# Attention heads laid out as two 64-row tensor tiles in place of zero-padded full-height tiles, with the maxima units regrouped by side

## The reference

```python
x = x + 0.5 * ffn(layernorm(x), ...)      # mixture of 8 experts, top 2, capacity 1.25
x = x + attn(layernorm(x), ...)           # below
x = x + 0.5 * ffn(layernorm(x), ...)      # the same experts again

def attn(x, wq, bq, wk, bk, wv, bv, wo, bo):          # x: (4, 1024, 128)
    q, k, v = (split(x @ w.T + b) for w, b in ...)    # 16 heads of width 8
    scores = einsum('bhsd,bhtd->bhst', q, k) / 8 ** 0.5
    scores = where(causal, scores, -inf)
    ctx = einsum('bhst,bhtd->bhsd', softmax(scores), v)
    return ctx.transpose(0, 2, 1, 3).reshape(B, S, E) @ wo.T + bo
```

## Time and profile before

| | us |
|---|---|
| median of three runs | 1189.49 |
| the profiled execution, span from first to last instruction | 1184.2 |
| median of the runs less that span | 5.3 |
| attention sweep with maxima (first scores of group 0 to first scores of group 15) | 380.7 to 907.7 |
| busy in the whole span: PE / DVE / ACT / POOL | 900.6 / 636.2 / 487.1 / 553.3 |

### The profile page before, as it was taken

How to read it: one execution, slowest core, us unless ns; L and a number is a source line. 1 busy time by engine, 2 the same in 40 slices (tenths; PEclk the granted TensorE clock), 3 DMA queues, 4 the chain that set the end, 5 groups by cost and what they waited for, 6 DMA issues and landing times. The chain is left out here.

```text
span 1184.2 us, 21961 instructions
## 1 busy us (share of the span) xinstructions
PE 900.6 (76%) x7525; PEld 560.8 (47%) x7525; DVE 636.2 (54%) x1515; ACT 487.1 (41%) x767; POOL 553.3 (47%) x645
## 2 busy tenths in 40 slices
PE   2320899992048999999999799999999622999980
PEld 2320677872023454555555355555554211878770
DVE  6440333331358878878777587787876130333230
ACT  1000343340021676568645477555766301443430
POOL 2775277767510322133427234163323632577776
PEclk9999999997566999999999899999999855999995
DMA  4212676733152114131152302422200113454522
GB/s 146 66 53 84 186 187 158 179 63 28 27 158 47 43 29 149 43 79 45 32 149 67 80 18 58 136 76 63 61 17 13 46 35 113 81 114 69 87 25 19
DMA packets 101649, 92.59 MB, mean 78 GB/s; under 512 B 15348, under 2 KB 80017, under 8 KB 101521
## 3 DMA queue, kind: packets, MB, share of 16 engines
q1 hardware_dynamic: 73024, 71.71, 21.8%
q0 software_dynamic: 27136, 17.09, 10.1%
q10 hardware_dynamic: 1392, 2.51, 0.7%
HBM read 48.32 MB, written 47.12 MB: 81 GB/s over the span
## 5 line engine op out<-in xcount | busy, mean ns | idle before, releaser
L1235 DVE TENSOR_REDUCE m_units<-banks 128x2 f32<-128x512 f32 (+1 forms) x576 | 381.1, 688 | 94.3 <-PE banks L954 78.6
L1184 ACT ACTIVATE pt<-banks 128x1024 f32<-128x1024 f32 (+3 forms) x384 | 291.4, 809 | 163.3 <-PE banks L937 161.4
L954 PE MATMUL banks<-kp,qa 128*128 128x256 bf16 (+1 forms) x1536 | 229.3, 254 | 17.7 <-DMA kp<-k_stack 10.3
L1444 POOL TENSOR_SCALAR_AFFINE_SELECT pt<-pt 128x512 f32<-128x512 f32 x128 | 81.6, 638 | 256.9 <-ACT pt L1184 256.7
L937 PE MATMUL banks<-qb,kp 128*128 128x512 bf16 (+3 forms) x768 | 188.6, 329 | 7.2 <-issue 5.1
L954 PEld LDWEIGHTS banks<-kp,qa 128*128 128x128 bf16 x1536 | 119.5, 99 | 148.7 <-DVE m_units L1235 59.5
L983 PE MATMUL banks<-pt,vs 128*32 128x256 f32 (+2 forms) x2560 | 178.5, 371 | 6.1 <-POOL pt L1444 6.0
L648 ACT ACTIVATE hT<-banks,bfc 128x512 f32<-128x512 f32 (+1 forms) x192 | 113.8, 615 | 168.4 <-DVE bfc L666 94.3
L722 POOL DMA_INDIRECT mid<-ys,ids x80 | 124.9, 1561 | 70.2 <-issue 34.4
L342 POOL DMA_INDIRECT bucket<-rows,row_ix x128 | 125.7, 982 | 64.2 <-issue 38.2
L722 POOL DMA_INDIRECT out_dram<-ys,ids x80 | 123.7, 1546 | 67.8 <-DVE ys L691 32.8
(11 more groups left out here) (166 smaller groups left out, 643.1 us busy)
## 6 DMA issues: line engine op xcount, KB each, us to landing
bucket<-zero SPq DMA_DIRECT2D x16, 660.0 KB, 4.2
xb<-bucket SPq DMA_DIRECT2D x16, 660.0 KB, 4.7
q_stack<-qp SPq DMA_DIRECT2D x24, 256.0 KB, 3.0
k_stack<-kq SPq DMA_DIRECT2D x24, 256.0 KB, 3.7
qa<-q_stack SPq DMA_DIRECT2D x32, 192.0 KB, 3.5
kp<-k_stack SPq DMA_DIRECT2D x32, 192.0 KB, 4.4
qb<-q_stack SPq DMA_DIRECT2D x32, 192.0 KB, 3.4
wfc<-in_L_ffn_c_fc_dram SPq DMA_DIRECT2D x16, 256.0 KB, 3.0
```

Source lines behind the costliest of these rows:

```text
L954: i = nc.tensor.matmul(a_bank[a % 2][:, j * w:(j + 1) * w], qa[par][:, h, qt * P:(qt + 1) * P], kp[g][:, h // 2, k0:k0 + w], start=not dia ...
L1184: nc.scalar.activation(pt[u % PTS][:, 2 * pair:2 * pair + 2, 0:w], two[pair][:, :, 0:w], ACT.Exp, scale=SCALE).then_inc(exp_done[pair], 1)
L1235: nc.vector.tensor_reduce(m_units[:, qt, at, heads[0]:heads[-1] + 1], a_bank[a % 2].rearrange("p (h k) -> p h k", k=w), AX.X, ALU.max).the ...
L1444: nc.gpsimd.affine_select(out=v, in_=v, compare_op=ALU.is_ge, fill=0.0, base=0, pattern=[[0, HS], [1, P]], channel_multiplier=-1).then_inc ...
```

## The change

- `qa` and `qb` hold two slabs (one per pair) where they held four. Side `s` of slab `i` is head `2i + s`, on partitions `64 s` and up. Nothing is zero-padded, and the four clears of `qa` and `qb` are gone.
- `score` and `maxima` take 51 or 48 rows, from partition 0 or 64, in both operands: each matmul is on one of two 64-row tiles. Banks, widths and the order of the blocks in a slot stay.
- A maxima unit has one side only: heads 0, 2 or heads 1, 3. A 256-key unit is two matmuls as before. The 128-key units and the diagonal units take two query tiles of one side where they took four heads of one query tile. The number of units stays 36, `A_IN_SLOT` stays, but the diagonal units now come last in each half. The reduce writes 2 heads of 1 or 2 query tiles.
- The transfers that fill `qb` from the maxima rows and `qa`, `qb` from the stacks keep their number and size; only the head order and the slab layout change.

```diff
+    HB = T // 2
     for hf in (1, 0):
-        for qt in range(hf * T // 2, (hf + 1) * T // 2):
+        qts = range(hf * HB, (hf + 1) * HB)
+        for qt in qts:
             for j in range(qt // 2):
-                AUNITS += [(qt, (0, 1), 2 * j * P, 2 * P, False, j), (qt, (2, 3), 2 * j * P, 2 * P, False, j)]
-            if qt % 2:
-                AUNITS.append((qt, range(HS), (qt - 1) * P, P, False, T // 2 - 1))
-            AUNITS.append((qt, range(HS), qt * P, P, True, T // 2))
+                for side in range(2):
+                    AUNITS.append((hf, side, [(qt, 2 * j * P)], 2 * P, False, j))
+        for side in range(2):
+            AUNITS.append((hf, side, [(qt, (qt - 1) * P) for qt in qts if qt % 2], P, False, HB - 1))
+        for q2 in range(hf * HB, (hf + 1) * HB, 2):
+            for side in range(2):
+                AUNITS.append((hf, side, [(q2, q2 * P), (q2 + 1, (q2 + 1) * P)], P, True, HB))
...
-            qa = [sba(f"qa{i}", [P, HS, S], bf16) for i in range(2)]
-            qb = [sba(f"qb{i}", [P, HS, S], bf16) for i in range(2)]
+            qa = [sba(f"qa{i}", [P, HS // 2, S], bf16) for i in range(2)]
+            qb = [sba(f"qb{i}", [P, HS // 2, S], bf16) for i in range(2)]
...
-                        i = nc.tensor.matmul(two[pair][:, s, 0:w], kp[g][:, pair, kb * P:(kb + 1) * P],
-                                             qb[par][:, 2 * pair + s, q0:q0 + w], start=True, stop=True)
+                        rows_s = slice(64 * s, 64 * s + KS + 3)
+                        i = nc.tensor.matmul(two[pair][:, s, 0:w], kp[g][rows_s, pair, kb * P:(kb + 1) * P],
+                                             qb[par][rows_s, pair, q0:q0 + w], start=True, stop=True)
...
-                        for j, h in enumerate(heads):
-                            i = nc.tensor.matmul(a_bank[a % 2][:, j * w:(j + 1) * w], qa[par][:, h, qt * P:(qt + 1) * P],
-                                                 kp[g][:, h // 2, k0:k0 + w], start=not diag,
-                                                 stop=not diag or j == len(heads) - 1)
+                        rows_s = slice(64 * side, 64 * side + KS)
+                        todo = [(qt, k0, pair) for qt, k0 in segs for pair in range(HS // 2)]
+                        for j, (qt, k0, pair) in enumerate(todo):
+                            i = nc.tensor.matmul(a_bank[a % 2][:, j * w:(j + 1) * w],
+                                                 qa[par][rows_s, pair, qt * P:(qt + 1) * P],
+                                                 kp[g][rows_s, pair, k0:k0 + w], start=not diag,
+                                                 stop=not diag or j == len(todo) - 1)
...
-                nc.vector.memset(qa[0][:], 0.0)
                 norm(0)
-                for t_ in qa[1:] + qb:
-                    i = nc.vector.memset(t_[:], 0.0)
-                i.then_inc(cleared, 1)
```

More of the change, by code:

```diff
@@ L830, in load_q @@
                 def load_q(dst, b, g, done):
-                    load_stack(lambda s: dst[64 * s:64 * s + KS].rearrange("p (i s) n -> p s i n", s=2)[:, s],
-                               q_stack, b, g, done)
+                    load_stack(lambda s: dst[64 * s:64 * s + KS], q_stack, b, g, done)
                 def load_k(b, g):
@@ L880, in move @@
                     for s in range(2):
[L881 to L884, removed]
+                        src = max_rows[hf * 3 * HS:(hf + 1) * 3 * HS, :].rearrange("(c s i) n -> s c i n", c=3, s=2)[s]
+                        dst = qb[par][64 * s + KS:64 * s + KS + 3]
+                        sp.dma_start(dst[:, :, hf * HALF:(hf + 1) * HALF], src).then_inc(max_ld[hf][par], 16)
                 def store_stacks(b):
@@ L914, in _ @@
                 wait_apart(sp, stack_st, STORES)
-                wait_apart(sp, cleared, 2)
+                wait_apart(sp, cleared, 1)
                 load_q(qa[0], 0, 0, qa_ld[0])
@@ L944, in maxima @@
                     for a in range(a0, a1):
-                        qt, heads, k0, w, diag, _ = AUNITS[a]
+                        _, side, segs, w, diag, _ = AUNITS[a]
                         if a == 0:
@@ L1099, in _ @@
                     norm_task(pro_at, name, 0)
-                pe.wait_ge(cleared, 2)
+                pe.wait_ge(cleared, 1)
                 maxima(0, 0, 0, 0, NA1 + 4)
@@ L1232, in reduce @@
                 def reduce(n, a):
-                    qt, heads, k0, w, diag, at = AUNITS[a]
+                    hf, side, segs, w, _, at = AUNITS[a]
+                    qt, apart = segs[0][0], segs[-1][0] - segs[0][0]
+                    if apart == 2:
+                        dst = m_units[:].rearrange("p (t o) c h -> p t o c h", o=2)[:, qt // 2:qt // 2 + 2, qt % 2, at]
+                    else:
+                        dst = m_units[:, qt:qt + apart + 1, at]
                     dve.wait_ge(a_full, NA * n + a + 1)
-                    nc.vector.tensor_reduce(m_units[:, qt, at, heads[0]:heads[-1] + 1],
-                                            a_bank[a % 2].rearrange("p (h k) -> p h k", k=w), AX.X,
+                    nc.vector.tensor_reduce(dst[:, :, 2 * side:2 * side + 2],
+                                            a_bank[a % 2].rearrange("p (t h k) -> p t h k", h=2, k=w), AX.X,
                                             ALU.max).then_inc(a_done, 1)
                     if a in (NA1 - 1, NA - 1):
-                        hf = int(a < NA1)
                         wait(dve, parts_ok, 2 * n - hf)
```

## The result

The changed kernel takes 1228.75 us, the median of four runs (1211.65 to 1235.79), against 1189.49 before. The ratio is 1.0249, 95% interval 1.0172 to 1.0325: slower, though whether by 2% stays open, where 1181 was forecast with 1214 as the upper end. Every ratio here leaves out executions that were clearly longer than the others of the same kernel (two of the four here; one of the kernel before took 1331.28 us at a clock of 0.741). The profiled execution is the longest of the four (span 1234.0 against 1184.2), so its 49.8 us of difference overstate the median's 39 by a quarter.

What follows compares the result with a forecast made beforehand. TensorE's issue order was taken to bound the sweep. -0.85 us per group over 15 groups (-13) and +5 for batch work took the 1184.2 span to 1176, plus 5.3 for the median: 1181 us, range 1151 to 1214.

Steps and rivals of the forecast that it cites:

- The scores: Score matmuls of a head pair in the sweep overlap on two row halves, halving 7.7 us: -3.85 us per plain group.
- C: Rival: the two halves of a score pair run one after the other, slower than before; +32, 1221 us; chance 16%.
- D: Rival: score pairs overlap only partly, two thirds of the gain (2.6 us per group); 1192 us; chance 10%.
- the part on the maxima: Both maxima matmuls of a unit share one tile and stay serial at 0.22 us: 0 gained per plain group.
- The change of row height: Switching between 128-row and 64-row matmuls, mainly around masks, costs 0.095 us each: +1.5 us per plain group at the masks.
- Rival B: Changes of row height are free, so masks and contexts cost nothing: about -38, 1151 us; chance 17%.
- The bank wait: With shorter scores, TensorE waits about 0.30 us for VectorE before a slot's second maxima unit: +1.2 us per plain group.
- The sum for a plain group: All terms for four heads without batch work in the sweep: -0.85 us, about 30.4 us against 31.3.
- the part on the extras: Groups with batch work have more full-height blocks, adding changes of row height: +1.7 us per batch, +5 in all.
- rival E: New waits let TensorE's clock fall to 1.2 GHz in the sweep; 60 us of it costs 25: 1207 us; chance 7%.
- Before the sweep: Removing the clears gains 0, 0.8 us at most; group 0's maxima with masks in a row cost +1 at most, taken as 0.
- The last group: Its scores at the end of the sweep already wait for ACT's exponentials, so the change gains 0.

Runs made afterwards that it cites:

- the two half-and-half runs: Only scores at half height, against the kernel before: 1199.46 us, ratio 1.0071; the changed kernel with scores back at full height, only maxima half: 1266.62 us, ratio 1.0627.
- the double masks: The changed kernel with 64 rows named in each score and maxima matmul, and each mask matmul issued twice: 1223.25 us, ratio 1.0285 to the kernel before.

## Why the prediction was wrong, point by point

- **The scores: right.** Pairs overlap: with the scores alone at half height, 0.33 us less the 0.10 of a border is 0.23, about half of 0.43. Rivals C and D are out. The overlap goes further than forecast: a maxima unit runs beside the scores of the other side (483.10 and 483.25 above), which the part on the maxima had ruled out by putting 0 there.
- **The change of row height: right in size.** 0.10 at the mask's borders and at every border of the two half-and-half runs, against 0.095. Rival B is out. The reading of the column changes held for rows too, which no row of the trace before had shown. The Trainium skill, TensorEngine Tiling (Array Packing), section Key Properties, says that changing the tiling mode drains TensorE; the traces agree, with 0.10 us at each change of height.
- **The bank wait: right where it is seen, in fewer slots.** 0.26 and 0.34 us where 0.30 was put; with a third one of 0.41 that makes 1.0 us in group 2, where 1.6 was put.
- **The sum for a plain group: right, and a little cautious.** 30.5 us for 30.4 (31.3 before), with 1.7 us of it at the lower clock; group 3, wholly at 2.4 GHz, is 1.5 shorter than before, where 0.85 was put. The group with norm and projections became 0.6 longer, and the part on the extras had put a loss there. Over the sweep the gain at the full clock is 17 us by the rough estimate above, where the forecast had 8.
- **The clock: wrong, and it is the step that failed.** The prediction named a falling clock (rival E), priced 60 us of it at 25, and gave it 7% with two reasons against: the sweep stays at 0.99, and 90% of the new slot is still work. Its sum had no term for the clock, and it named the price of a change of row height as what would most easily make it wrong. It took busy time for what the clock follows. The first reason was a row of a kernel whose matmuls all named 128 rows, zeros included; the second counts time alone. The runs show a busy TensorE kept at 1.2 GHz for 48 us at 48 and 51 rows and for 58 us at 32. The length was off threefold, 171 us of the sweep and not 60, and the cost with it, about 59 us by the estimate above and not 25.
- **What the zero padding was worth.** The padding was listed as removed and priced by its clears (0 us). The runs with 64 and with 66 rows show that naming rows of zeros is part of what held the clock.
- **Before the sweep.** The profiled execution reached its first scores 4.5 us later (385.2 against 380.7), where 0 was put and 1.8 at most. The run with 64 rows, with the same masks, is at 380.5, and the one with 32 rows at 380.3. So neither the order nor the row count alone makes it; its cause stays open. The last group, put at 0, became 3.6 us longer, which was not followed up either.

Not settled: why the clock falls in one slot and not in another. Falls come mostly in slots 9 to 11 and where TensorE waits for the router's chain, but the double masks did not hold it and spreading them moved it. That the rows named count is shown by the step from 48 and 51 to 64 rows and by the one from 128 to 66 at a full-height tile, and the run with 32 rows goes the same way; how they are weighed is not, and the double masks, which added full-height work and hardly moved the clock, leave it open.

## What to carry to other kernels

Before giving up zero rows or unused height in TensorE's stream, ask what they do for its clock: read the granted clock of the stretch, and try the edit with rows padded back to the tile's end first. A half-height tile is worth using where pairs of matmuls lie together and neighbours have the same height; each border costs 0.10 us, and here confining it to the wide slots, with 64 rows named, turned a loss of 2.5% into a gain of 1.6%, of which half a percent is the order's. A forecast that halves the array's work should carry the lower clock as a main case and not as a mishap.

## What the runs showed of the hardware that was not expected

- The granted clock depends on how many rows matmuls name, with columns and order equal: 0.754 at 32, 0.848 at 48 and 51 (0.864 in its fastest execution), 0.886 at 64. At full-height tiles, 66 rows gave 0.861, where the kernel before has 0.902 to 0.908 on the same chip; 128 rows in the same order gave 0.921 on a chip where it has 0.916 to 0.920 in most executions.
- At 1.2 GHz a group of 30.5 us takes 46.5, not 61. A wide slot with values blocks takes 4.48 us there (396.18 to 400.66) and 3.02 at 2.4 GHz (481.27 to 484.29). The wait of 0.26 us for VectorE is gone in it and a border still costs about 0.1; the rest was not followed up.
- Matmuls on different row halves overlap across kinds of work (scores beside maxima), not only inside a pair, where banks differ.
